# First layer's selective scan: decay kept in SBUF, B and C spread 1024 columns at a time, six of 48 y additions moved to VectorE

## The chip, the cores and the metric

The kernel runs on one core of one Trainium2 chip, as one launch. The metric is the device time in microseconds (us); three runs of the kernel before gave 1568.59 to 1570.61 with a median of 1569.81. TensorE does the matrix products, VectorE, ScalarE and GpSimd work on 128 partitions of SBUF (GpSimd reaches SBUF alone, the other two PSUM as well), and each engine runs its own instructions in order; semaphores tie the engines together. In the profile's rows PE is TensorE, PEld its weight load, DVE VectorE, ACT ScalarE, POOL GpSimd and SP the engine that issues most DMAs.

## The reference

A two-layer image model on an input of 4 x 48 x 64 x 64. The first layer's mixer is a selective scan in four directions (rows forward and back, columns forward and back) over 4096 positions, 96 channels, one state per channel. The change touches only this part:

```python
dts = jnp.einsum('bkrl,kdr->bkdl', dts_r, dt_projs_weight)
delta = jax.nn.softplus(dts + dt_projs_bias[None, :, :, None])
dA = jnp.exp(delta[..., None] * A[None, :, :, None, :])
dBu = delta[..., None] * Bt[:, :, None] * xs[..., None]
# h[t] = dA[t] * h[t-1] + dBu[t], by an associative scan
y = jnp.einsum('bkdln,bkln->bkdl', hs, Ct) + Ds.reshape(K, D_INNER)[None, :, :, None] * xs
# the four directions are turned back to image order and added up
```

After it come a norm, a projection, a small quantized feed-forward block, and the second layer (convolution, a 16-state scan, projection, feed-forward), which the change leaves alone.

## The kernel before

The program is five phases, one after the other: `front0_phase` (norm, convolution, the small projections), `scan0_phase` (this scan), `back0_phase`, `mid1_phase` (the second layer with its own, larger scan) and `back1_phase`.

`scan0_phase` puts 4 images x 32 channels on the 128 partitions and passes three times (`j`, J = 3) over the 96 channels. In each pass it walks four directions in the order of `order` (line 855): direction 2 (rows, backward), 1 (columns, forward), 3 (columns, backward), 0 (rows, forward). A direction is cut into NTC = 4 pieces of TC = 1024 positions. One piece in one direction is a *step*; there are 3 x 4 x 4 = 48 steps, 24 in row order and 24 in column order. A column step reads `z` and adds into `y` with a stride of 64 elements (`seen`, line 866), and has its own tiles in column order.

One step `i` goes like this:

- TensorE: two matmuls of 512 columns give the time step (`dt_of`, into `q_dt`), and two each spread B and C over the partitions (`spread`, into `q_b` and `q_c`, one bank of 512 columns each, so that the second half waits until VectorE has read the first).
- ScalarE: Softplus of `q_dt` into `dl` (`delta_of`), then Exp of `dl` times a per-channel scale into `q_a` (`decay`), which lies in PSUM, two buffers of 1024. It does two steps at a time, since the two functions need different tables.
- GpSimd: `u = dl * z` (line 1110), and two steps later `y += g` (line 1121). Both read two tiles of SBUF.
- VectorE: `u = u * q_b` in two halves (`drive`, line 1051), the scan `h` over 1024 positions from `q_a` and `u` (line 1062), and `g = h * q_c` of the step before in two halves (`times_c`, line 1073). Each of these reads one tile of SBUF and one of PSUM; where a direction goes on, the scan also takes its start value from the last column of the other `h`.

VectorE's order is written out (lines 1080 to 1088): first half of drive(i), first half of times_c(i-1), the second halves, then scan(i). GpSimd's is u(i), then y(i-2). `u`, `h`, `g` and `q_a` have two buffers, `dl` four, so u(i) waits for scan(i-2) and the product g(i) for y(i-2). `y` starts as `z` times a sum of D (`begin_y`, on ScalarE), and leaves by DMA after its last direction.

Of the kernel before, what the change touches and what calls it, by code (L numbers as in the profile page):

```python
# [21 lines left out]
ALU = mybir.AluOpType  # L22
# [808 lines left out]
def scan0_phase(nc, D, G, sems, past):  # L831

    with ExitStack() as scope:
# [14 lines left out]
        (y_begun, a_exp, a_ready, d_ready, dt_mm, b_mm, c_mm,  # L848
         delta, da_ready, u_ready, driven, scanned, read, added, y_stored) = (
            m.sem(f"b_{n}") for n in (  # L850
                "y_begun", "a_exp", "a_ready", "d_ready",
                "dt_mm", "b_mm", "c_mm", "delta", "da_ready", "u_ready", "driven", "scanned",
                "read", "added", "y_stored"))
# [31 lines left out]
        def from_rows(ap, col):  # L885

            return ap.rearrange("p (h w) -> p w h", h=H) if col else ap

        def by_column(ap, col):

            return ap.rearrange("p (w h) -> p w h", h=H) if col else ap
# [2 lines left out]

            return 2 * i + v + 1 + LEAD

        def in_order(back):

            return ((0, 1), (1, 0)) if back else ((0, 0), (1, 1))

        @block.sync
        def _(sp):
            def load_dt(k):
                for g, part in enumerate(X_PARTS):
                    sp.dma_start(dtx[k][DTR * g:DTR * g + DTR, :], D["dt0"][part, :, R0 * k:R0 * k + R0, :]).then_inc(dt_loaded[k], 16)
                sp.dma_start(dtx[k][BIAS_ROW:BIAS_ROW + 3, :], D["ones"].broadcast_to([3, T])).then_inc(dt_loaded[k], 16)

            def load_z(j):
                sp.dma_start(z[j % 2][:], D["z0"][j]).then_inc(z_loaded[j % 2], 16)

            def store(j):

                for c in range(NTC):
                    sp.wait_ge(added, done(n * j + 3 * NTC + c))
# [12 lines left out]
            load_z(1)  # L927
            for j in range(J):
                if j + 2 < J:
                    sp.wait_ge(u_ready, j * n + n + LEAD)  # L930
                    sp.wait_ge(y_begun, NTC * j + NTC)
                    load_z(j + 2)
                store(j)
            sp.wait_ge(y_stored, 16 * NTC * J)
            sp.nop(nofuse=True)

        @block.tensor
        def _(pe):
# [19 lines left out]
            def spread(j, st, o, q, row, used, ready):  # L958

                k, col, back, piece, first = steps[st]  # L960
                v = in_order(back)[o][1]

                if j * n + st < NTC:
                    pe.wait_ge(bc_first[piece], 16)
                pe.wait_ge(used, half(j * n + st, o) - 1)
                nc.tensor.matmul(in_rows(q[:], col), G["selbc0"][:, row + k, :],  # L966
                                 seen_rows(bcx[:], col, piece, v), start=True, stop=True).then_inc(ready, 1)

            def ahead(i, by):
                if i + by < last:  # L970
                    dt_of(i + by)

            dt_of(0)
            dt_of(1)
# [68 lines left out]
        def _(dve):  # L1043
            lead(dve, driven, scanned, read)

            def drive(i, s, o, v):
                part, col = slice(v * CH, v * CH + CH), steps[i % n][1]
                dve.wait_ge(u_ready, done(i))
                dve.wait_ge(b_mm, half(i, o))
                half_u = by_column(u[s][:, part], col)  # L1050
                nc.vector.tensor_tensor(half_u, half_u, from_rows(q_b[:], col), ALU.mult).then_inc(driven, 1)  # L1051

            def scan(i, s, back, first):
                way = slice(None, None, -1) if back else slice(None)
                dve.wait_ge(driven, half(i, 1))
                dve.wait_ge(da_ready, done(i))

                dve.wait_ge(scanned, done(i - 1))

                dve.wait_ge(read, half(i - 2, 1))  # L1060
# [4 lines left out]
            def times_c(i, o):  # L1065
                col, s = steps[i % n][1], i % 2
                v = in_order(steps[i % n][2])[o][1]
                part = slice(v * CH, v * CH + CH)
                dve.wait_ge(scanned, done(i))
                dve.wait_ge(c_mm, half(i, o))  # L1070

                dve.wait_ge(added, freed(i))
                nc.vector.tensor_tensor(by_column(g[s][:, part], col), by_column(h[s][:, part], col), from_rows(q_c[:], col),  # L1073
                                        ALU.mult).then_inc(read, 1)
# [12 lines left out]
            for o in range(2):  # L1087
                times_c(last - 1, o)

        @block.gpsimd  # L1090
        def _(pool):
# [7 lines left out]
            for i in range(last + 2):  # L1099
                if i < last:  # L1100
# [5 lines left out]
                    elif st == 0:  # L1106
# [1072 lines left out]
```

## Time and profile before

| | us |
|---|---|
| median of three runs | 1569.81 |
| the profiled execution | 1570.93 |
| its span in the profile | 1569.0 |
| first scan of this phase starts | 217.87 |
| last y addition of this phase ends | 474.23 |
| GpSimd busy from 236.7 to 466.6 | 229.90 |
| VectorE busy from 236.7 to 466.6 | 208.43 |
| ScalarE busy from 236.7 to 466.6 | 157.06 |
| TensorE busy from 236.7 to 466.6 | 136.29 |

The span is the stretch that the profiler recorded, 1.9 us less than the execution's own time, and that execution was 1.1 us above the median of the runs. TensorE's granted clock is 0.50 of full speed in all of the scan phase, the lower of its two levels. The last rows of the table add up what each engine was busy within a stretch; an engine that is busy for the whole of a stretch bounds it, one that is not waits for something. A duration in the trace holds everything from an instruction's start to its end, so one that has to wait after it has started shows the wait as part of its duration. Back-to-back instructions overlap a little: the time from the start of one to the start of the next is what one of them costs in a row of them.

### The profile page before, as it was taken

How to read it: one execution, taken by the hardware profiler on the slowest of the kernel's cores; microseconds unless marked ns; L12 is line 12 of the kernel's file. 1: busy time of each engine (PE TensorE's matmuls, PEld its weight loads, DVE VectorE, ACT ScalarE, POOL GpSimd, SP SyncE). 2: the span in 40 equal slices, each digit the busy share in tenths (PEclk: the TensorE clock that was granted, in tenths of full speed). 3: DMA queues.
4: the chain of work that ended last, by engine and by line, in shares of the span. 5: the costliest groups of instructions: out<-in, count | busy, mean ns of one | idle time of the engine just before them, and what ended most of it. 6: DMA issues, size and time to landing. Idle time of an engine off the chain costs nothing. (4 is left out here: it accounts for less than half of the span.)

```text
span 1569.0 us, 14783 instructions
## 1 busy us (share of the span) xinstructions
PE 1155.8 (74%) x3828; PEld 423.9 (27%) x3828; DVE 1205.6 (77%) x1198; ACT 1107.2 (71%) x1643; POOL 947.1 (60%) x501
## 2 busy tenths in 40 slices
PE   4899636665643777777888888888888888455995
PEld 2343101111102555422222222222222222002663
DVE  1666539998982777604999999999999999992775
ACT  2687257767642777648889889888888888741664
POOL 2500059999993333216988988888888889850000
PEclk8999855555556999978888888888888888666997
DMA  5455450301002233218878777788777886616572
GB/s 144 123 145 141 98 173 17 108 0 41 14 28 86 84 94 100 76 45 213 191 181 190 183 173 171 178 187 185 177 171 180 183 186 158 155 44 131 127 176 56
DMA packets 137487, 200.56 MB, mean 128 GB/s; under 512 B 27099, under 2 KB 69130, under 8 KB 136916
## 3 DMA queue, kind: packets, MB, share of 16 engines
q1 hardware_dynamic: 133964, 193.27, 50.1%
q0 software_dynamic: 1280, 3.74, 0.8%
q10 hardware_dynamic: 2160, 2.61, 0.7%
q8 instruction: 32, 0.52, 0.1%
q14 instruction: 51, 0.42, 0.1%
HBM read 145.93 MB, written 53.63 MB: 127 GB/s over the span
## 5 line engine op out<-in xcount | busy, mean ns | idle before, releaser
L1802 DVE TENSOR_TENSOR_SCAN m_h<-m_qa,m_state,m_ub 128x512 f32<-128x512 f32 x384 | 464.1, 1263 | 63.7 <-POOL m_ub L1389 56.9
L1389 POOL TENSOR_TENSOR m_ub<-m_dlb,m_bt 128x1536 f32<-128x1536 f32 x128 | 440.4, 3441 | 16.5 <-DMA m_dlb<-scratch_dldu 6.0
L1753 ACT ACTIVATE m_qa<-m_dlb,k_a 128x512 f32<-128x512 f32 x384 | 250.9, 681 | 56.7 <-DVE m_h L1802 52.1
L1813 DVE TENSOR_TENSOR m_g<-m_h,m_qc 128x1536 f32<-128x1536 f32 x128 | 221.4, 1730 | 10.0 <-DVE m_h L1802 8.6
L1596 PE MATMUL m_qm<-m_xa,k_u_taps 96*96 96x512 f32 x192 | 152.3, 959 | 32.3 <-ACT m_sz L1681 31.6
L1635 PE MATMUL m_qy<-m_g,k_seld 128*32 128x512 f32 x768 | 157.9, 697 | 0.0
L1110 POOL TENSOR_TENSOR b_u<-b_dl,b_z 128x1024 f32<-128x1024 f32 x48 | 130.3, 2714 | 17.9 <-ACT b_dl L1000 16.1
L1121 POOL TENSOR_TENSOR b_y<-b_y,b_g 128x1024 f32<-128x1024 f32 x48 | 135.9, 2830 | 3.4 <-DVE b_g L1073 3.2
L1618 PE MATMUL m_qc<-m_cp,k_selc 112*128 112x512 bf16 x128 | 52.3, 409 | 105.7 <-DVE m_g L1813 105.7
L966 PE MATMUL b_qb<-b_bc,k_pack_sel 96*128 96x512 bf16 x96 | 58.9, 613 | 94.8 <-DVE b_u L1051 94.7
L1411 POOL TENSOR_TENSOR m_rest<-m_bcr,m_cp 16x512 f32<-16x512 f32 x32 | 36.9, 1152 | 105.3 <-ACT m_cp L1722 76.1
L1051 DVE TENSOR_TENSOR b_u<-b_u,b_qb 128x512 f32<-128x512 f32 x96 | 65.3, 680 | 43.3 <-PE b_qb L966 29.8
L536 PE MATMUL n_q<-a_cv,k_conv 113*96 113x504 f32 (+1 forms) x192 | 91.9, 620 | 5.9 <-DVE a_acc L555 5.9
L1550 PE MATMUL m_qf<-m_cva,k_conv 113*96 113x504 f32 (+1 forms) x192 | 91.5, 614 | 4.9 <-PEq L1141 4.9
L1007 ACT ACTIVATE b_qa<-b_dl,b_a 128x1024 f32<-128x1024 f32 x48 | 53.6, 1118 | 58.5 <-DVE b_h L1062 58.3
L1062 DVE TENSOR_TENSOR_SCAN b_h<-b_qa,b_h,b_u 128x1024 f32<-128x1024 f32 x36 | 84.3, 2343 | 0.0
L1596 PEld LDWEIGHTS m_qm<-m_xa,k_u_taps 96*96 96x96 f32 x192 | 45.8, 257 | 138.8 <-issue 137.3
L1095 POOL DMA_DIRECT2D b_bc<-scratch_bc x4 | 2.3, 586 | 127.1 <-POOLq L577 127.1
L955 PE MATMUL b_qdt<-b_dt,b_wdt 75*128 75x512 bf16 x96 | 51.5, 622 | 33.2 <-DMA b_dt<-scratch_dt 24.5
L1000 ACT ACTIVATE b_dl<-b_qdt 128x512 f32<-128x512 f32 x96 | 52.1, 595 | 23.3 <-PE b_qdt L955 21.9
L1073 DVE TENSOR_TENSOR b_g<-b_h,b_qc 128x512 f32<-128x512 f32 x96 | 65.2, 679 | 1.0 <-PE b_qc L966 0.8
L1618 PEld LDWEIGHTS m_qc<-m_cp,k_selc 112*128 112x128 bf16 x128 | 12.9, 101 | 190.1 <-issue 188.3
(191 smaller groups left out, 2350.5 us busy)
## 6 DMA issues: line engine op xcount, KB each, us to landing
m_dlb<-scratch_dldu SPq DMA_DIRECT2D x128, 384.0 KB, 9.9
m_bt<-scratch_brow SPq DMA_DIRECT2D x128, 256.0 KB, 5.8
scratch_dldu<-m_dldu SPq DMA_DIRECT2D x32, 384.0 KB, 3.2
scratch_z<-a_z SPq DMA_DIRECT2D x24, 256.0 KB
scratch_y<-b_y SPq DMA_DIRECT2D x12, 512.0 KB, 2.6
c_y<-scratch_y SPq DMA_DIRECT2D x16, 384.0 KB, 3.4
scratch_gate<-m_gt SPq DMA_DIRECT2D x32, 192.0 KB, 3.7
scratch_y<-m_yo SPq DMA_DIRECT2D x32, 192.0 KB, 11.5
```

Of the source, the lines that this page charges most:

```text
L536: last = self.nc.tensor.matmul(out[:, :, o], self.pairs[:, tap, :], src[:, :, i], start=(tap == 1), stop=(tap == 2))
L1051: nc.vector.tensor_tensor(half_u, half_u, from_rows(q_b[:], col), ALU.mult).then_inc(driven, 1)
L1062: nc.vector.tensor_tensor_scan(h[s][:, way], q_a[s][:, way], u[s][:, way], carried, ALU.mult, ALU.add).then_inc(scanned, 1)
L1110: nc.gpsimd.tensor_tensor(by_column(u[s][:], col), by_column(dl[i % DL][:], col), seen(z[j % 2][:], col, piece), ALU.mult).then_inc(u_read ...
L1121: nc.gpsimd.tensor_tensor(part, part, by_column(g[i % 2][:], col), ALU.add).then_inc(added, 1)
L1389: nc.gpsimd.tensor_tensor(ub[k % 3][:], dlb[u % 2][:, J:2 * J, :], bcast(bt[u % 2][:, n, :], J), ALU.mult).then_inc(ub_ready, 1)
L1550: nc.tensor.matmul(out[:, :, o], G["conv1"][:, tap, :], src[:, :, i], start=(tap == 1), stop=False)
L1596: last = nc.tensor.matmul(q_m[:], G["u_taps"][:, k, :], xa[v % HIST][:, k:k + CH], start=(k == 0), stop=(k == 2))
L1635: last = nc.tensor.matmul(q_y[32 * j:32 * j + 32, :], G["seld"][:], g[k % 2][:, j, :], start=(n == 0), stop=(n == 3))
L1753: nc.scalar.activation(q_a[:, j, :], dlb[u % 2][:, j, :], ACT.Exp, scale=G["a1"][:, j, n:n + 1]).then_inc(da, 1)
L1802: nc.vector.tensor_tensor_scan(h[k % 3][:, j, :], q_a[:, j, :], ub[k % 3][:, j, :], state[:, k % NS, j:j + 1], ALU.mult, ALU.add).then_inc ...
L1813: nc.vector.tensor_tensor(g[k % 2][:], h[k % 3][:], bcast(q_c[:], J), ALU.mult).then_inc(read, 1)
```

## The change

Four edits, all in `scan0_phase`. The decay `qa` becomes an SBUF tile (two buffers of 1024). The four banks of PSUM that this frees make `q_b` two buffers of 1024 columns and `q_c` one of 1024. TensorE spreads B and C for a whole step (two matmuls, one signal), and B one step ahead. VectorE's drive and times_c become one instruction of 1024 each. And of the four steps of a column direction, the third one's `y += g` is done by VectorE (`add_y`, after scan(i+1)) and left out on GpSimd, with a semaphore of its own (`summed`): 2 column directions x 3 passes = 6 of 48 additions.

```diff
-        q_dt = m.ps("b_qdt", [P, TC])
-        q_b, q_c = m.ps("b_qb", [P, CH]), m.ps("b_qc", [P, CH])
-        q_a = [m.ps(f"b_qa{s}", [P, TC]) for s in range(2)]
+        qa = [m.sb(f"b_qa{s}", [P, TC]) for s in range(2)]
+        q_dt, q_c = m.ps("b_qdt", [P, TC]), m.ps("b_qc", [P, TC])
+        q_b = [m.ps(f"b_qb{s}", [P, TC]) for s in range(2)]
...
+        def by_vector(i):
+
+            return steps[i % n][1] and i % NTC == 2
...
+        def wait_direction(eng, i):
+
+            before = i - i % NTC - 1
+            if before >= 0:
+                eng.wait_ge(added, adds(before))
+                if sums(before) > 0:
+                    eng.wait_ge(summed, sums(before))
...
             for i in range(last + 1):
-                for o in range(2):
-                    if i < last:
-                        spread(i // n, i % n, o, q_b, 0, driven, b_mm)
-                    if i > 0:
-                        spread((i - 1) // n, (i - 1) % n, o, q_c, K4, read, c_mm)
-                    if o == 0 and i % 2 == 1:
-                        ahead(i, 2)
-                if i == 0:
+                b_of(i + 1)
+                if i == 0 or i % 2 == 1:
                     ahead(i, 2)
+                if i > 0:
+                    c_of(i - 1)
                 if i % 2 == 1:
                     ahead(i, 3)
...
-                nc.scalar.activation(q_a[i % 2][:], dl[i % DL][:], ACT.Exp, scale=a0[:, j, k:k + 1]).then_inc(da_ready, 1)
+                nc.scalar.activation(qa[i % 2][:], dl[i % DL][:], ACT.Exp, scale=a0[:, j, k:k + 1]).then_inc(da_ready, 1)
...
-                nc.vector.tensor_tensor_scan(h[s][:, way], q_a[s][:, way], u[s][:, way], carried,
+                nc.vector.tensor_tensor_scan(h[s][:, way], qa[s][:, way], u[s][:, way], carried,
                                              ALU.mult, ALU.add).then_inc(scanned, 1)
...
+            def add_y(i):
+                if not by_vector(i):
+                    return
+                k, col, back, piece, first = steps[i % n]
+                wait_direction(dve, i)
+                dve.wait_ge(read, done(i))
+                part = seen(y[i // n % 2][:], col, piece)
+                nc.vector.tensor_tensor(part, part, by_column(g[i % 2][:], col), ALU.add).then_inc(summed, 1)
...
-                for o, v in in_order(back):
-                    drive(i, i % 2, o, v)
-                    if i > 0:
-                        times_c(i - 1, o)
+                drive(i, i % 2)
+                if i > 0:
+                    times_c(i - 1)
                 scan(i, i % 2, back, first)
+                if i > 0:
+                    add_y(i - 1)
...
-                if i >= 2:
+                if i >= 2 and not by_vector(i - 2):
...
+                    wait_direction(pool, i - 2)
+                    if adds(i - 2) > LEAD + 1:
+                        pool.wait_ge(added, adds(i - 2) - 1)
```

On VectorE, at the end of the first column direction (steps 7 and 8): `b_u` is the driven input, `b_h` the scan's result, `b_g` the product with C, numbers are buffers, `b_qa` the decay, and the scan is listed as SCALAR_TENSOR_TENSOR. Before:

```order
L1051 TENSOR_TENSOR b_u1<-b_u1,b_qb 128x512 [waits b_b_mm,b_u_ready]
L1073 TENSOR_TENSOR b_g0<-b_h0,b_qc 128x512 [waits b_added,b_c_mm,b_scanned]
L1051 TENSOR_TENSOR b_u1<-b_u1,b_qb 128x512 [waits b_b_mm,b_u_ready]
L1073 TENSOR_TENSOR b_g0<-b_h0,b_qc 128x512 [waits b_added,b_c_mm,b_scanned]
L1062 SCALAR_TENSOR_TENSOR b_h1<-b_qa1,b_h0,b_u1 128x1024 [waits b_scanned,b_read,b_da_ready,b_driven]
```

The same place after the change, up to the next scan:

```order
L1087 TENSOR_TENSOR b_u1<-b_u1,b_qb1 128x1024 [waits b_b_mm,b_u_ready]
L1108 TENSOR_TENSOR b_g0<-b_h0,b_qc 128x1024 [waits b_added,b_c_mm,b_scanned]
L1098 SCALAR_TENSOR_TENSOR b_h1<-b_qa1,b_h0,b_u1 128x1024 [waits b_scanned,b_read,b_da_ready,b_driven]
L1118 TENSOR_TENSOR b_y0<-b_y0,b_g0 128x16x64 [waits b_read,b_added]
L1087 TENSOR_TENSOR b_u0<-b_u0,b_qb0 128x1024 [waits b_b_mm,b_u_ready]
L1108 TENSOR_TENSOR b_g1<-b_h1,b_qc 128x1024 [waits b_added,b_c_mm,b_scanned]
L1098 SCALAR_TENSOR_TENSOR b_h0<-b_qa0,b_u0 128x1024 [waits b_scanned,b_read,b_da_ready,b_driven]
```

Four half instructions became two whole ones, and the addition for step 6 stands behind scan(7). On GpSimd, over the same steps, before:

```order
L1121 TENSOR_TENSOR b_y0<-b_y0,b_g1 128x16x64 [waits b_added,b_read]
L1110 TENSOR_TENSOR b_u0<-b_dl0,b_z0 128x1024 [waits b_scanned,b_delta]
L1121 TENSOR_TENSOR b_y0<-b_y0,b_g0 128x16x64 [waits b_added,b_read]
L1110 TENSOR_TENSOR b_u1<-b_dl1,b_z0 128x1024 [waits b_scanned,b_delta]
L1121 TENSOR_TENSOR b_y0<-b_y0,b_g1 128x16x64 [waits b_added,b_read]
```

And with the change:

```order
L1167 TENSOR_TENSOR b_y0<-b_y0,b_g1 128x16x64 [waits b_added,b_read]
L1154 TENSOR_TENSOR b_u0<-b_dl0,b_z0 128x1024 [waits b_scanned,b_delta]
L1154 TENSOR_TENSOR b_u1<-b_dl1,b_z0 128x1024 [waits b_scanned,b_delta]
L1167 TENSOR_TENSOR b_y0<-b_y0,b_g1 128x16x64 [waits b_added,b_read]
L1154 TENSOR_TENSOR b_u0<-b_dl2,b_z0 128x1024 [waits b_scanned,b_delta]
```

Between the products for steps 8 and 9 the addition for step 6 is gone; everything else keeps its place. On TensorE, at an odd step (`b_qdt` is the time step's product, two matmuls), with the change:

```order
L995 MATMUL b_qb0<-b_bc,k_pack_sel 128x512 [waits b_driven]
L995 MATMUL b_qb0<-b_bc,k_pack_sel 128x512
L986 MATMUL b_qdt<-b_dt1,b_wdt 128x512 [waits b_delta] x2
L995 MATMUL b_qc<-b_bc,k_pack_sel 128x512 [waits b_read]
L995 MATMUL b_qc<-b_bc,k_pack_sel 128x512
L986 MATMUL b_qdt<-b_dt3,b_wdt 128x512 [waits b_delta,b_dt_loaded3]
```

There both matmuls of C stand behind a time-step product that waits for ScalarE; before, the first half of C stood ahead of it.

## Rows read from the trace of the kernel before

**Rows 1.** Busy time of each engine in the steady stretch (by --windows; x counts instructions).
```profile
core 0: us, PE busy (x) PEld busy (x) DVE busy (x) ACT busy (x) POOL busy (x), PEclk, DMA share, GB/s
236.70:466.60 229.90, 136.29 (x257) 26.32 (x256) 208.43 (x219) 157.06 (x178) 229.90 (x88) 0.50 0.09 33
```
**Rows 2.** GpSimd's timeline: start, duration, line, operation; idle before in brackets.
```profile
244.12 2.85 POOL L1110 TENSOR_TENSOR b_u<-b_dl,b_z 128x1024 f32<-128x1024 f32 x1
...
252.81 3.06 POOL L1121 TENSOR_TENSOR b_y<-b_y,b_g 128x1024 f32<-128x1024 f32 x1
255.83 2.84 POOL L1110 TENSOR_TENSOR b_u<-b_dl,b_z 128x1024 f32<-128x1024 f32 x1
...
279.14 2.41 POOL L1110 TENSOR_TENSOR b_u<-b_dl,b_z 128x1024 f32<-128x1024 f32 x1
...
289.80 2.42 POOL L1110 TENSOR_TENSOR b_u<-b_dl,b_z 128x1024 f32<-128x1024 f32 x1
...
317.49 2.95 POOL L1110 TENSOR_TENSOR b_u<-b_dl,b_z 128x1024 f32<-128x1024 f32 x1
...
471.89 2.34 POOL L1121 TENSOR_TENSOR b_y<-b_y,b_g 128x1024 f32<-128x1024 f32 x1 [2.10 <-DVE b_g L1073]
```
**Rows 3.** Waits from 226 to 467: who waited for whom, us, times, longest.
```profile
ACT b_qa L1007 <- DVE b_h L1062: 58.3, 23, 3.5
...
DVE b_u L1051 <- POOL b_u L1110: 13.5, 22, 0.9
DVE b_u L1051 <- PE b_qb L966: 8.7, 46, 0.8
```
**Rows 4.** VectorE's groups from 226 to 467: count, busy us, mean ns, idle before.
```profile
L1062 DVE TENSOR_TENSOR_SCAN b_h<-b_qa,b_h,b_u 128x1024 f32<-128x1024 f32 x35 | 82.0, 2343 | 0.0
L1051 DVE TENSOR_TENSOR b_u<-b_u,b_qb 128x512 f32<-128x512 f32 x92 | 62.6, 680 | 22.2 <-POOL b_u L1110 13.5 <-PE b_qb L966 8.7
L1073 DVE TENSOR_TENSOR b_g<-b_h,b_qc 128x512 f32<-128x512 f32 x92 | 62.5, 679 | 0.3 <-issue 0.3
```
**Rows 5.** VectorE's timeline: the second scan and the next instruction.
```profile
225.72 2.34 DVE L1062 TENSOR_TENSOR_SCAN b_h<-b_qa,b_h,b_u 128x1024 f32<-128x1024 f32 x1
227.99 0.66 DVE L1051 TENSOR_TENSOR b_u<-b_u,b_qb 128x512 f32<-128x512 f32 x1
```
**Rows 6.** The second layer's scan and GpSimd product: ns min/median/max.
```profile
L1802 DVE TENSOR_TENSOR_SCAN m_h<-m_qa,m_state,m_ub x384: 1251/1258/1284, 728.2 to 1411.0; 128x512 f32<-128x512 f32 x192
...
L1389 POOL TENSOR_TENSOR m_ub<-m_dlb,m_bt x128: 3410/3442/3472, 724.6 to 1396.8; 128x1536 f32<-128x1536 f32 x128
```
**Rows 7.** Line 555, first phase: ns min/median/max; n_q is PSUM, a_acc and a_low SBUF.
```profile
L555 DVE SCALAR_TENSOR_TENSOR a_acc<-a_low,k_pack_d,a_acc x64: 737/740/3453, 46.2 to 184.4; 96x504 f32<-96x504 f32 x64
L555 DVE SCALAR_TENSOR_TENSOR a_acc<-a_low,k_pack_d,n_q x32: 730/744/746, 45.4 to 182.9; 96x512 f32<-96x512 f32 x32
```
**Rows 8.** Timeline, first phase: one such VectorE instruction and the GpSimd one beside it.
```profile
47.44 3.40 POOL L200 TENSOR_TENSOR dtw<-dtw,dt_part 13x1536 f32<-13x1536 f32 x1
...
47.93 3.45 DVE L555 SCALAR_TENSOR_TENSOR a_acc<-a_low,k_pack_d,a_acc 96x504 f32<-96x504 f32 x1
```
**Rows 9.** Third phase: line 1286 overall (ns min/median/max), then a timeline; tiles in SBUF.
```profile
L1286 DVE TENSOR_TENSOR c_y<-c_y,c_yrs x16: 945/1444/1469, 491.1 to 645.0; 128x768 f32<-128x768 f32 x16
...
624.30 0.72 POOL L1169 TENSOR_TENSOR c_ys<-c_y 128x256 f32<-128x256 f32 x1 [2.44 <-DMA c_xin<-in_x]
624.65 1.19 DVE L1286 TENSOR_TENSOR c_y<-c_y,c_yrs 128x768 f32<-128x768 f32 x1 [0.16 <-ACT c_yrs L1270]
625.11 1.32 POOL L1171 TENSOR_TENSOR c_ys<-c_ys,c_y 128x256 f32<-128x256 f32 x1
```
**Rows 10.** VectorE products of 1536 and 1024 columns, one input in PSUM: mean ns.
```profile
L1813 DVE TENSOR_TENSOR m_g<-m_h,m_qc 128x1536 f32<-128x1536 f32 x128 | 221.4, 1730 | 10.0 <-DVE m_h L1802 8.6 <-issue 0.8
...
L1906 DVE TENSOR_TENSOR g_y<-g_q,g_gt 96x1024 f32<-96x1024 f32 x16 | 19.4, 1213 | 24.9 <-PE g_q L1875 24.9
```

More of the change, by code:

```diff
@@ L844, in scan0_phase @@
         u, h, g = ([m.sb(f"b_{n}{s}", [P, TC]) for s in range(2)] for n in ("u", "h", "g"))
-        q_dt = m.ps("b_qdt", [P, TC])
-        q_b, q_c = m.ps("b_qb", [P, CH]), m.ps("b_qc", [P, CH])
-        q_a = [m.ps(f"b_qa{s}", [P, TC]) for s in range(2)]
+        qa = [m.sb(f"b_qa{s}", [P, TC]) for s in range(2)]
+        q_dt, q_c = m.ps("b_qdt", [P, TC]), m.ps("b_qc", [P, TC])
+        q_b = [m.ps(f"b_qb{s}", [P, TC]) for s in range(2)]
         (y_begun, a_exp, a_ready, d_ready, dt_mm, b_mm, c_mm,
-         delta, da_ready, u_ready, driven, scanned, read, added, y_stored) = (
+         delta, da_ready, u_ready, driven, scanned, read, added, summed, y_stored) = (
             m.sem(f"b_{n}") for n in (
@@ L852, in scan0_phase @@
                 "dt_mm", "b_mm", "c_mm", "delta", "da_ready", "u_ready", "driven", "scanned",
-                "read", "added", "y_stored"))
+                "read", "added", "summed", "y_stored"))
         order = [(2, 0, 1), (1, 1, 0), (3, 1, 1), (0, 0, 0)]
@@ L887, in from_rows, with halves_from_rows, halves_by_column @@
             return ap.rearrange("p (h w) -> p w h", h=H) if col else ap
+        def halves_from_rows(ap, col):
+            return ap.rearrange("p (v h w) -> p v w h", v=TC // CH, h=H) if col else ap
+        def halves_by_column(ap, col):
+            return ap.rearrange("p (v w h) -> p v w h", v=TC // CH, h=H) if col else ap
         def by_column(ap, col):
@@ L895, in half, with sums, adds, wait_added @@
             return 2 * i + v + 1 + LEAD
-        def in_order(back):
-            return ((0, 1), (1, 0)) if back else ((0, 0), (1, 1))
+        def by_vector(i):
+            return steps[i % n][1] and i % NTC == 2
+        def sums(i):
+            return sum(by_vector(e) for e in range(i + 1))
+        def adds(i):
+            return LEAD + i + 1 - sums(i)
+        def wait_added(eng, i):
+            if by_vector(i):
+                eng.wait_ge(summed, sums(i))
+            else:
+                eng.wait_ge(added, adds(i))
+        def wait_direction(eng, i):
[4 more added lines that the diff above has]
+                    eng.wait_ge(summed, sums(before))
         @block.sync
@@ L913, in store @@
                 for c in range(NTC):
-                    sp.wait_ge(added, done(n * j + 3 * NTC + c))
+                    wait_added(sp, n * j + 3 * NTC + c)
                     sp.nop(nofuse=True)
@@ L956, in dt_of, with spread, b_of, c_of @@
                                      seen_rows(dtx[k][:], col, piece, v), start=True, stop=True).then_inc(dt_mm, 1)
[L958 to L963, printed above, removed]
+            def spread(i, q, row, ready):
+                k, col, back, piece, first = steps[i % n]
+                if i < NTC:
                     pe.wait_ge(bc_first[piece], 16)
-                pe.wait_ge(used, half(j * n + st, o) - 1)
-                nc.tensor.matmul(in_rows(q[:], col), G["selbc0"][:, row + k, :],
-                                 seen_rows(bcx[:], col, piece, v), start=True, stop=True).then_inc(ready, 1)
+                for v in range(TC // CH):
+                    last = nc.tensor.matmul(in_rows(q[:, v * CH:v * CH + CH], col), G["selbc0"][:, row + k, :],
+                                            seen_rows(bcx[:], col, piece, v), start=True, stop=True)
+                last.then_inc(ready, 1)
+            def b_of(i):
+                if i < last:
+                    pe.wait_ge(driven, freed(i))
+                    spread(i, q_b[i % 2], 0, b_mm)
+            def c_of(i):
+                pe.wait_ge(read, freed(i, 1))
+                spread(i, q_c, K4, c_mm)
             def ahead(i, by):
@@ L973, in _ @@
             dt_of(0)
+            b_of(0)
             dt_of(1)
             for i in range(last + 1):
[L976 to L983 removed]
+                b_of(i + 1)
+                if i == 0 or i % 2 == 1:
                     ahead(i, 2)
+                if i > 0:
+                    c_of(i - 1)
                 if i % 2 == 1:
@@ L1044, in _, with drive @@
             lead(dve, driven, scanned, read)
-            def drive(i, s, o, v):
-                part, col = slice(v * CH, v * CH + CH), steps[i % n][1]
+            def drive(i, s):
+                col = steps[i % n][1]
                 dve.wait_ge(u_ready, done(i))
-                dve.wait_ge(b_mm, half(i, o))
-                half_u = by_column(u[s][:, part], col)
-                nc.vector.tensor_tensor(half_u, half_u, from_rows(q_b[:], col), ALU.mult).then_inc(driven, 1)
+                dve.wait_ge(b_mm, done(i))
+                whole_u = halves_by_column(u[s][:], col)
+                nc.vector.tensor_tensor(whole_u, whole_u, halves_from_rows(q_b[s][:], col), ALU.mult).then_inc(driven, 1)
@@ L1053, in scan @@
             def scan(i, s, back, first):
                 way = slice(None, None, -1) if back else slice(None)
-                dve.wait_ge(driven, half(i, 1))
+                dve.wait_ge(driven, done(i))
                 dve.wait_ge(da_ready, done(i))
                 dve.wait_ge(scanned, done(i - 1))
-                dve.wait_ge(read, half(i - 2, 1))
+                dve.wait_ge(read, done(i - 2))
                 carried = 0.0 if first else h[1 - s][:, 0:1] if back else h[1 - s][:, TC - 1:TC]
-                nc.vector.tensor_tensor_scan(h[s][:, way], q_a[s][:, way], u[s][:, way], carried,
+                nc.vector.tensor_tensor_scan(h[s][:, way], qa[s][:, way], u[s][:, way], carried,
@@ L1063, in scan, with times_c @@
                                              ALU.mult, ALU.add).then_inc(scanned, 1)
-            def times_c(i, o):
+            def times_c(i):
                 col, s = steps[i % n][1], i % 2
-                v = in_order(steps[i % n][2])[o][1]
-                part = slice(v * CH, v * CH + CH)
                 dve.wait_ge(scanned, done(i))
[L1070 to L1074, printed above, removed]
+                dve.wait_ge(c_mm, done(i))
+                if i >= 2:
+                    wait_added(dve, i - 2)
+                nc.vector.tensor_tensor(halves_by_column(g[s][:], col), halves_by_column(h[s][:], col),
+                                        halves_from_rows(q_c[:], col), ALU.mult).then_inc(read, 1)
@@ L1076, in _ @@
+            def add_y(i):
+                if not by_vector(i):
+                    return
+                k, col, back, piece, first = steps[i % n]
+                wait_direction(dve, i)
+                dve.wait_ge(read, done(i))
+                part = seen(y[i // n % 2][:], col, piece)
+                nc.vector.tensor_tensor(part, part, by_column(g[i % 2][:], col), ALU.add).then_inc(summed, 1)
             dve.wait_ge(a_loaded, 32)
@@ L1081, in _ @@
                 back, first = steps[i % n][2], steps[i % n][4]
-                for o, v in in_order(back):
-                    drive(i, i % 2, o, v)
-                    if i > 0:
-                        times_c(i - 1, o)
+                drive(i, i % 2)
+                if i > 0:
+                    times_c(i - 1)
                 scan(i, i % 2, back, first)
-            for o in range(2):
-                times_c(last - 1, o)
+                if i > 0:
+                    add_y(i - 1)
+            times_c(last - 1)
         @block.gpsimd
@@ L1116, in _ @@
                         pool.wait_ge(y_begun, NTC * j + st + 1)
-                    pool.wait_ge(read, half(i - 2, 1))
-                    pool.wait_ge(added, done(i - 3))
+                    pool.wait_ge(read, done(i - 2))
+                    wait_direction(pool, i - 2)
+                    if adds(i - 2) > LEAD + 1:
+                        pool.wait_ge(added, adds(i - 2) - 1)
                     part = seen(y[j % 2][:], col, piece)
```

## The prediction, made before the run

> **What bounds the kernel now.** I read the busy times of the scan stretch first, then GpSimd's timeline, the waits and VectorE's groups, and last the places elsewhere in the program where VectorE and GpSimd meet on SBUF tiles.
>
> From 236.7 to 466.6 us GpSimd is busy for all 229.90 us of 229.90, VectorE for 208.43, ScalarE for 157.06, TensorE for 136.29 [rows 1]. So GpSimd sets the pace of this phase, and its timeline gives its prices, start to start [rows 2]. In a row stretch, from 289.80 to 317.49, stand 12 instructions: 27.69 / 12 = 2.31 us each. In a column stretch, from 244.12 to 279.14, stand six pairs: 35.02 / 6 = 5.84 a pair, of which the addition takes 255.83 - 252.81 = 3.02 and the product `u` the other 2.82. The last addition ends at 471.89 + 2.34 = 474.2.
>
> The others wait for it or for what it feeds: VectorE's drive waits 13.5 us for `u`, ScalarE's Exp 58.3 us for a scan [rows 3]. VectorE's scan takes 2.34 us, 2.27 from its start to the next instruction's [rows 4, 5], a half product 0.68. In a step it has 2.27 and four halves, no more than 5.0 us: under GpSimd's 5.84 in column steps, a little over its 2.31 x 2 = 4.62 in row steps.
>
> **The change, part by part.** *Whole products.* Of 1024 columns with one PSUM input a product takes about 1.21 us [rows 10], and 1.73 at 1536 columns. Two per step are 2.42 for 4 x 0.68 = 2.72: 0.30 x 48 = 14 us less VectorE time. It lies beside GpSimd's work and gains nothing while GpSimd is the bound.
>
> *B and C spread ahead.* The number of matmuls stays. The 8.7 us that VectorE waited for B [rows 3] can go; GpSimd is late next, so nothing by itself. If GpSimd were not the cover, this and the whole products would be worth 8.7 and 14 us in VectorE's row steps at most.
>
> *New waits.* `add_y(i)` waits for the additions of the direction before; on GpSimd those stand ahead of u(i), which VectorE needed for its drive(i) long before. GpSimd's first addition of a direction waits for the VectorE addition of the one before; VectorE does that ahead of the product g which the same GpSimd addition needs anyway. Neither can end last, so what is queued behind them (the next `u`, the next drive) is not held.
>
> *Six additions leave GpSimd.* 6 x 3.02 = 18.1 us off the bound. On VectorE each is a 1024-column sum with strided y. No row shows one: below it stands 1.21 (contiguous, rows 10), above it GpSimd's own 3.06 [rows 2]. I take 1.21 x 3.02 / 2.31 = 1.6, VectorE's price with the factor that the stride costs GpSimd: 9.6 us for six.
>
> The Trainium skill, "Vector Engine (DVE) Microarchitecture Reference", section 5.2, gives 1.7 to 2.5 ns a column where an operand hops every element; as an estimate that is 1.8 to 2.6 us each, and the sum below would rise by 1 to 6 us. No run here shows it.
>
> *The decay in SBUF.* This is what I expect to decide the time. Before, the scan read one SBUF tile (`u`) and one PSUM tile. Now it reads two SBUF tiles, and so does `add_y`. GpSimd's two instructions always read two. What the trace shows of such pairs:
>
> - One SBUF input beside GpSimd: no effect. The second layer's scans run from 1251 to 1284 ns while GpSimd's products run beside them in 3410 to 3472 [rows 6]; this phase's half products average 680 and 679 [rows 4].
> - Two SBUF inputs: line 555 with PSUM as one input takes 730 to 746 ns in every case, with both in SBUF 737 to 3453 [rows 7]. The 3.45 us one starts at 47.93, in a GpSimd instruction that ends at 50.84, and ends at 51.38, 0.54 after it [rows 8]. Alone it takes 0.74, so it stood still for nearly all of the GpSimd instruction.
> - The other way round too: line 1286, 0.945 us alone, starts at 624.65, waits for the GpSimd addition that ends at 625.02 and ends at 625.84; the next GpSimd addition, issued at 625.11, takes 1.32 instead of 0.72 and ends 0.59 after VectorE's [rows 9]. The one that waited got in between two GpSimd instructions.
>
> So the two exclude each other for whole instructions. The Trainium skill, "SBUF — State Buffer", section "Who interferes with whom", says just that: a VectorE instruction with two SBUF inputs contends with a GpSimd one that reads SBUF, and whichever comes second is fully blocked. By that rule the scan must take turns with GpSimd, and the trace agrees for the two operations with such rows (3.45 against 0.74 us); of a scan it has no row with two SBUF inputs.
>
> If the scans take turns with GpSimd, the phase lasts as long as the sum of both, whatever the order. In every step the scan leaves GpSimd a `u` and a `y` to do, and VectorE's two products (2.42 us) fit beside one or the other, so the shared resource doesn't fall idle; whether VectorE gets in after one GpSimd instruction or after two, a step costs scan + u + y: 2.27 + 4.62 = 6.89 in row steps, 2.27 + 5.84 = 8.11 in column steps. TensorE and ScalarE, at 136 and 157 us of 230, stay hidden, and the C product's later place costs nothing.
>
> The sum, from the second scan's start at 225.72, which I leave where it is (up to there the change adds one C matmul, tenths of a us): 47 scans x 2.27 = 106.7; GpSimd's 21 `u` and 24 `y` of row steps x 2.31 = 104.0; 24 column pairs x 5.84 = 140.2; less 18.1; six VectorE additions 9.6. Together 342.4. The last addition ends at 225.7 + 342.4 = 568.1 instead of 474.2: 93.9 us later. What follows is unchanged. The profiled execution took 1570.9, so 1664.8; it lay 1.1 over the median of the runs, which gives 1664.
>
> Its bounds. Down: in the blocked cases part of the duration was already spent while waiting, 0.54 shown of 0.74 [rows 7, 8] and 0.59 of 0.72 [rows 9]. A scan then holds 2.34 - 0.20 = 2.14 (6 us less over 47), one GpSimd instruction a step 2.34 - 0.13 = 2.21 (5 less), an addition 1.21 (2 less): 1651. Up: full durations instead of start to start, 0.07 x 47 + 0.03 x 93 = 6; additions at 3.06, 9 more; a wake-up of 0.16 a step, as VectorE shows behind ScalarE [rows 9], 8 more: 1687.
>
> **Rivals.** *Faster: the scan is not held.* One mechanism, at line 1098, and it decides for all 47 scans at once: a scan uses two ns per column, so its second input may come another way than that of a product. For it: no row shows such a scan, and all scans so far ran undisturbed [rows 4, 6]. Against it: line 555 is also a two-step operation on two SBUF tiles and was held. GpSimd then stays the bound with 18.1 us less to do; VectorE needs 2.27 + 2.42 in a row step, like GpSimd: 1569.8 - 18.1 = 1552. Chance 0.08.
>
> *No change: the scan is not held, but C comes late.* In odd steps both C matmuls now stand behind a time-step product that waits for Softplus. If VectorE waited there as long as its longest wait for B, 0.8 us [rows 3], in 24 odd steps, 19 us would eat the 18.1. It decides only where GpSimd has no slack left. 1570; chance 0.02.
>
> *Half the price: they slow each other down instead of taking turns.* Then half of the scans' and additions' 116.3 us might be lost: 1552 + 58 = 1610. For it: a scan asks for a column only every 2 ns. Against it: rows 8 and 9 show standing still and no slowing. Chance 0.05.
>
> **How the numbers follow.** Forecast (turns taken) 0.85, range 1651 to 1687. A measurement of this kernel can tell 0.2%, some 3 us, from no change. Slower by more: 0.85 + 0.05 = 0.90; faster 0.08; within 0.02. The range for 8 in 10 has to take nearly all of the first case, so I widen its bounds a little, 1640 to 1692; the half price and the two cases without a hold stay outside.
>
> **What would show it.** In the changed profile the scan's mean should rise from 2.34 to between 3 and 5 us with maxima near 2.3 + 3, and GpSimd's `u` and `y` from 2.7 and 2.8 towards 4, both with waiting inside their durations; drive and times_c should stay at 1.2. `add_y` should show several us where a GpSimd instruction runs. GpSimd should still look busy throughout a phase that is some 94 us longer, and every other phase should keep its length. I would be wrong if scans stay at 2.34 beside GpSimd (then the time is near 1552), if scans lengthen but GpSimd's instructions do not and it has idle time (then it is another wait), or if the phase is longer while VectorE waits for C.

## The result, and the profile after

The changed kernel takes **1653.18 us** (median of 4 runs, 1649.85 to 1655.67) beside 1570.21 for the kernel before in the same series: a ratio of **1.0521, with 95% interval 1.049 to 1.0553**. It is slower by 83 us, where 94 were forecast, and inside the range. The profiled execution took 1651.93 us, its span is 1650.0.

All of it lies in the scan phase. The last `y` addition ended at 474.23 before and ends at 554.44 + 2.34 = 556.78 now, 82.6 us later; from there to the end of the span it was 1094.8 us before and is 1093.2 now.

Busy time of each engine in the steady stretch, 313.20 us long, as in [rows 1]:

```profile
core 0: us, PE busy (x) PEld busy (x) DVE busy (x) ACT busy (x) POOL busy (x), PEclk, DMA share, GB/s
236.70:549.90 313.20, 121.94 (x253) 22.64 (x252) 282.55 (x139) 157.22 (x178) 312.53 (x82) 0.50 0.06 23
```

GpSimd looks as full as before, 312.53 of 313.20, yet needs 83 us more for less work. Which instructions became longer is in the groups of the stretch from 226 to 556 (count, busy us, mean ns, idle us before and its releaser):

```profile
L1167 POOL TENSOR_TENSOR b_y<-b_y,b_g 128x1024 f32<-128x1024 f32 x42 | 169.3, 4032 | 1.4 <-DVE b_g L1108 1.2 <-POOL b_y L1167 0.2
L1154 POOL TENSOR_TENSOR b_u<-b_dl,b_z 128x1024 f32<-128x1024 f32 x45 | 164.7, 3665 | 0.0
L1098 DVE TENSOR_TENSOR_SCAN b_h<-b_qa,b_h,b_u 128x1024 f32<-128x1024 f32 x36 | 130.5, 3626 | 0.0
L1108 DVE TENSOR_TENSOR b_g<-b_h,b_qc 128x1024 f32<-128x1024 f32 x47 | 56.8, 1208 | 0.0
L1087 DVE TENSOR_TENSOR b_u<-b_u,b_qb 128x1024 f32<-128x1024 f32 x46 | 55.1, 1198 | 30.7 <-POOL b_u L1154 30.7
```

The scan rose from a mean of 2343 ns [rows 4] to 3626; GpSimd's two kinds, 2.34 to 3.06 us before [rows 2], to means of 4032 and 3665. VectorE's products, which read one PSUM input, are at their 1.2 us. No new wait explains it: GpSimd, which sets the pace, is idle for 1.4 us. VectorE waits 30.7 us for `u` (13.5 before) and not at all for B or C, ScalarE's Exp 121.7 us for scans (58.3 before [rows 3]). The loss is inside the durations. The smallest, median and largest of each (ns), by line:

```profile
L1098 DVE TENSOR_TENSOR_SCAN b_h<-b_qa,b_h,b_u x36: 2340/2892/4956, 224.8 to 549.8; 128x1024 f32<-128x1024 f32 x36
...
L1118 DVE TENSOR_TENSOR b_y<-b_y,b_g x6: 4341/4597/4853, 267.9 to 525.0; 128x1024 f32<-128x1024 f32 x6
...
L1154 POOL TENSOR_TENSOR b_u<-b_dl,b_z x48: 2332/3548/4882, 209.6 to 543.1; 128x1024 f32<-128x1024 f32 x48
...
L1167 POOL TENSOR_TENSOR b_y<-b_y,b_g x42: 2337/4342/5083, 225.0 to 554.4; 128x1024 f32<-128x1024 f32 x42
```

The smallest of the scans and of GpSimd's two kinds is the old price, the largest that price and most of the other engine's instruction on top. The timeline of a row stretch shows how one runs into the other (start, duration, engine, line, operation):

```profile
316.31 2.34 POOL L1154 TENSOR_TENSOR b_u<-b_dl,b_z 128x1024 f32<-128x1024 f32 x1
316.34 4.47 DVE L1098 TENSOR_TENSOR_SCAN b_h<-b_qa,b_h,b_u 128x1024 f32<-128x1024 f32 x1
318.62 4.34 POOL L1167 TENSOR_TENSOR b_y<-b_y,b_g 128x1024 f32<-128x1024 f32 x1
320.72 1.19 DVE L1087 TENSOR_TENSOR b_u<-b_u,b_qb 128x1024 f32<-128x1024 f32 x1
321.84 1.21 DVE L1108 TENSOR_TENSOR b_g<-b_h,b_qc 128x1024 f32<-128x1024 f32 x1
322.92 2.34 POOL L1154 TENSOR_TENSOR b_u<-b_dl,b_z 128x1024 f32<-128x1024 f32 x1
322.97 4.44 DVE L1098 TENSOR_TENSOR_SCAN b_h<-b_qa,b_h,b_u 128x1024 f32<-128x1024 f32 x1
...
349.33 2.85 POOL L1154 TENSOR_TENSOR b_u<-b_dl,b_z 128x1024 f32<-128x1024 f32 x1
```

The scan of 316.34 starts while `u` runs. `u` ends at 318.65, the scan at 320.81, 2.16 us after it. `y`, issued at 318.62, stands still meanwhile and ends at 322.96, 2.15 after the scan; beside it VectorE does its two products at full speed. Then the pattern repeats. From 316.31 to 349.33 are five steps: 6.60 us each, where GpSimd alone took 2 x 2.31 = 4.62 [rows 2]. So a scan adds 1.98.

### The profile page after: what moved, and what is told of

It is laid out like the page before. It is cut to its first block and busy times, and to the rows that moved or that the text cites. A ratio compares the mean times of both kernels' runs of the same rounds, so it can differ in the third digit from the quotient of the medians.

```text
span 1650.0 us, 14619 instructions
## 1 busy us (share of the span) xinstructions
PE 1151.3 (70%) x3828; PEld 420.8 (26%) x3828; DVE 1279.1 (78%) x1108; ACT 1107.8 (67%) x1643; POOL 1033.5 (63%) x495
## 3 DMA queue, kind: packets, MB, share of 16 engines
q10 hardware_dynamic: 2160, 2.61, 0.7%
## 5 line engine op out<-in xcount | busy, mean ns | idle before, releaser
L1799 ACT ACTIVATE m_qa<-m_dlb,k_a 128x512 f32<-128x512 f32 x384 | 250.8, 681 | 54.5 <-DVE m_h L1848 50.5
L1154 POOL TENSOR_TENSOR b_u<-b_dl,b_z 128x1024 f32<-128x1024 f32 x48 | 171.7, 3582 | 17.2 <-ACT b_dl L1036 15.0
L1642 PE MATMUL m_qm<-m_xa,k_u_taps 96*96 96x512 f32 x192 | 156.2, 981 | 30.3 <-ACT m_sz L1727 29.6
L1167 POOL TENSOR_TENSOR b_y<-b_y,b_g 128x1024 f32<-128x1024 f32 x42 | 169.3, 4032 | 1.4 <-DVE b_g L1108 1.2
L995 PE MATMUL b_qb<-b_bc,k_pack_sel 96*128 96x512 bf16 x96 | 49.8, 622 | 169.6 <-DVE b_u L1087 169.6
L1681 PE MATMUL m_qy<-m_g,k_seld 128*32 128x512 f32 x768 | 162.8, 716 | 0.0
L1043 ACT ACTIVATE b_qa<-b_dl,b_a 128x1024 f32<-128x1024 f32 x48 | 55.0, 1149 | 121.9 <-DVE b_h L1098 121.7
L1098 DVE TENSOR_TENSOR_SCAN b_h<-b_qa,b_h,b_u 128x1024 f32<-128x1024 f32 x36 | 130.5, 3626 | 0.0
L1087 DVE TENSOR_TENSOR b_u<-b_u,b_qb 128x1024 f32<-128x1024 f32 x48 | 57.5, 1199 | 45.8 <-POOL b_u L1154 45.8
L1215 POOL TENSOR_TENSOR c_ys<-c_ysq 128x256 f32<-128x256 f32 x16 | 11.6, 724 | 82.6 <-ACT c_ysq L1310 82.6
```

The lines of the kernel that those rows point to most:

```text
L1098: nc.vector.tensor_tensor_scan(h[s][:, way], qa[s][:, way], u[s][:, way], carried, ALU.mult, ALU.add).then_inc(scanned, 1)
L1642: last = nc.tensor.matmul(q_m[:], G["u_taps"][:, k, :], xa[v % HIST][:, k:k + CH], start=(k == 0), stop=(k == 2))
L1681: last = nc.tensor.matmul(q_y[32 * j:32 * j + 32, :], G["seld"][:], g[k % 2][:, j, :], start=(n == 0), stop=(n == 3))
L1799: nc.scalar.activation(q_a[:, j, :], dlb[u % 2][:, j, :], ACT.Exp, scale=G["a1"][:, j, n:n + 1]).then_inc(da, 1)
```

## The experiments

The phase's start shifts by up to 5 us between executions, for reasons ahead of it, so beside the totals I give the phase's length in the profiled execution, from GpSimd's first `u` to the end of the last `y`. Ratios are to the kernel before on the same chip, where its median was 1567.81 us (1 to 4), 1569.28 (5 to 7) and 1570.96 (8 and 9).

| kernel | us | ratio, 95% interval | phase, us |
|---|---|---|---|
| before | 1570.21 | 1 | 262.9 |
| after | 1653.18 | 1.0521 (1.049 to 1.0553) | 347.1 |
| 1 only the decay in SBUF | 1659.88 | 1.0579 (1.0553 to 1.0606) | 353.9 |
| 2 after, no VectorE additions | 1655.96 | 1.0564 (1.0532 to 1.0596) | 353.1 |
| 3 after, driven input in PSUM | 1573.78 | 1.0038 (1.0014 to 1.0062) | 266.4 |
| 4 as 3, no VectorE additions | 1564.88 | 0.9981 (0.9967 to 0.9995) | 260.8 |
| 5 before, with VectorE additions | 1576.67 | 1.0029 (1.0007 to 1.0052) | 269.7 |
| 6 as 3, added product in PSUM | 1557.56 | 0.9901 (0.9867 to 0.9935) | 248.6 |
| 7 as 3, addition ahead of the scan | 1575.91 | 1.0029 (1.0007 to 1.005) | 267.0 |
| 8 as 6, `u` freed by the drive | 1552.75 | 0.9887 (0.9869 to 0.9905) | 246.9 |
| 9 as 8, nine additions | 1557.36 | 0.9922 (0.9895 to 0.9949) | 250.8 |

**1. Only the decay in SBUF.** One line of the kernel before:

```diff
-        q_a = [m.ps(f"b_qa{s}", [P, TC]) for s in range(2)]
+        q_a = [m.sb(f"b_qa{s}", [P, TC]) for s in range(2)]
```

> The kernel before with one edit: the decay tile in SBUF instead of PSUM; half products, single B and C banks and all 48 additions on GpSimd stay. Theory (a scan with two SBUF inputs takes turns with GpSimd): in the changed kernel a row step lasted 6.60 us, so a scan holds GpSimd up for 6.60 - 4.62 = 1.98; 47 x 1.98 = 93 us on top of GpSimd's 244, end of the phase near 563 instead of 474: about 1659. Rival (the time of the changed kernel comes from its whole-step spreads, the later C product or the additions on VectorE): no difference, 1570, scans at 2.34.

1659.88: this line alone brings the whole loss. The scans by line (ns, smallest, median, largest):

```profile
L1062 DVE TENSOR_TENSOR_SCAN b_h<-b_qa,b_h,b_u x36: 2345/2514/7858, 225.9 to 558.1; 128x1024 f32<-128x1024 f32 x36
L1062 DVE TENSOR_TENSOR_SCAN b_h<-b_qa,b_u x12: 2284/2494/4567, 218.0 to 536.9; 128x1024 f32<-128x1024 f32 x12
```

The median is only 0.17 above the old price: here it is mostly GpSimd that stands still. One scan waited for longer than any in the changed kernel, 7.86 us; its place in the timeline:

```profile
410.68 3.14 POOL L1121 TENSOR_TENSOR b_y<-b_y,b_g 128x1024 f32<-128x1024 f32 x1
...
413.41 7.86 DVE L1062 TENSOR_TENSOR_SCAN b_h<-b_qa,b_h,b_u 128x1024 f32<-128x1024 f32 x1
...
413.73 2.38 POOL L1110 TENSOR_TENSOR b_u<-b_dl,b_z 128x1024 f32<-128x1024 f32 x1
416.02 3.10 POOL L1121 TENSOR_TENSOR b_y<-b_y,b_g 128x1024 f32<-128x1024 f32 x1
...
421.41 2.35 POOL L1110 TENSOR_TENSOR b_u<-b_dl,b_z 128x1024 f32<-128x1024 f32 x1 [2.29 <-DVE b_h L1062]
```

It began while a `y` ran, which ended at 413.82. Then `u` and the next `y` went ahead of it at their full speed, and it ended 2.15 after the second (419.12, 421.27). GpSimd, with nothing left that it could do before this scan's end, was idle for 2.29. That cost little: from the `u` of 413.73 two steps last 15.22 us, and the same two steps of the other passes 14.65 and 14.63. So a scan that lets two instructions pass costs 0.6 us more here, close to the nothing that the prediction had for it.

**2. All additions back on GpSimd.** After, with one line changed:

```diff
-            return steps[i % n][1] and i % NTC == 2
+            return False
```

> The changed kernel with all 48 additions back on GpSimd; decay in SBUF and whole products stay. Theory: an addition on VectorE holds GpSimd up for about 1.5 us and saves it 3.02, so giving six back costs 6 x 1.5 = 9 us: about 1662. Rival (the 4.3 to 4.9 us that these additions show are time on the path): 6 x (4.6 - 3.0) = 10 us less, about 1643.

The totals, 1655.96 and 1653.18, don't tell the two kernels apart, and they match neither number expected. The phase does tell them apart, 353.1 beside 347.1, but in one profiled execution of each, and that of 2 is the slowest of its four (1663.35 us). The step lengths of the two traces agree with it: with an addition on VectorE, two steps take 14.54 us in the first column direction (265.78 to 280.32) and 13.67 in the second, without it 15.66 and 14.62. So six additions moved to VectorE save 6.0 us, 1.0 each: 3.02 on GpSimd against 2.0 of excluded time on VectorE, where 1.5 was expected. Whole products and the early B and C, all that is left between kernels 1 and 2, are worth 353.9 - 353.1 = 0.8 at most, about the nothing that was forecast; about 0.6 of it is the long scan of 1.

**3. The driven input in PSUM.** After, with decay still in SBUF; `q_b` gives up a buffer, and the C matmuls go ahead of the next B:

```diff
-        q_b = [m.ps(f"b_qb{s}", [P, TC]) for s in range(2)]
+        q_b, q_u = m.ps("b_qb", [P, TC]), m.ps("b_qu", [P, TC])
...
+                if i > 0:
+                    dve.wait_ge(scanned, done(i - 1))
-                nc.vector.tensor_tensor(whole_u, whole_u, halves_from_rows(q_b[s][:], col), ALU.mult).then_inc(driven, 1)
+                nc.vector.tensor_tensor(halves_by_column(q_u[:], col), whole_u, halves_from_rows(q_b[:], col), ALU.mult).then_inc(driven, 1)
...
-                nc.vector.tensor_tensor_scan(h[s][:, way], qa[s][:, way], u[s][:, way], carried,
+                nc.vector.tensor_tensor_scan(h[s][:, way], qa[s][:, way], q_u[:, way], carried,
```

> The changed kernel, but VectorE writes the driven input (u times B) to a PSUM tile, so that the scan reads one SBUF tile (the decay) and one PSUM tile; B has one buffer of 1024 columns instead of two, and C is spread ahead of the next B. Theory: it is the number of SBUF inputs that counts, so scans are back at 2.34 and GpSimd is the bound with 18 us less to do, of which the additions on VectorE still hold it up for 9: about 1561. Rival (the decay in SBUF or the whole-step spreads cost the time in another way): near 1650. A third outcome: with one buffer of B VectorE waits about 1.2 us a step for it: about 1595.

The 83 us are gone, but the time missed 1561 by 13: the additions, which still read two SBUF tiles, gave their gain back. Their durations, and the first of them with GpSimd's timeline:

```profile
L1122 DVE TENSOR_TENSOR b_y<-b_y,b_g x6: 2930/5696/6221, 259.7 to 453.2; 128x1024 f32<-128x1024 f32 x6
```

```profile
258.18 2.86 POOL L1158 TENSOR_TENSOR b_u<-b_dl,b_z 128x1024 f32<-128x1024 f32 x1
...
259.74 6.22 DVE L1122 TENSOR_TENSOR b_y<-b_y,b_g 128x1024 f32<-128x1024 f32 x1
...
260.99 2.86 POOL L1158 TENSOR_TENSOR b_u<-b_dl,b_z 128x1024 f32<-128x1024 f32 x1
...
268.28 3.08 POOL L1171 TENSOR_TENSOR b_y<-b_y,b_g 128x1024 f32<-128x1024 f32 x1 [4.43 <-DVE b_g L1112]
```

It started in the first `u`, and the second went ahead of it, both unhindered at 2.86. The addition ended 2.11 after the second one; VectorE's next product came after it, and GpSimd had to wait 4.43 for `g`. GpSimd's waits for `g` are 21.2 us in all, more than the 18.1 saved.

**4. As 3, no VectorE additions** (the edit of 2).

> As the kernel with the driven input in PSUM, but all 48 additions on GpSimd. No VectorE instruction of the phase then has two SBUF inputs. Theory: GpSimd is the bound with the work that it had before, 1570, and the whole products gain nothing since they lie beside it. Rival (VectorE was the bound in row steps, where it had 5.0 us against 4.6): up to 24 x 0.3 = 7 us less, 1563.

1564.88, between the two numbers expected and nearer the rival's. The rival's reason isn't borne out: GpSimd's 12 instructions from 288.46 to 316.18 take 27.72 us, as the 12 before took 27.69 [rows 2]. Of the 2.1 us by which the phase is shorter than before, 1.6 lie behind GpSimd's last `u`, where GpSimd waits for VectorE's last scan and product. The scans:

```profile
L1102 DVE TENSOR_TENSOR_SCAN b_h<-b_qa,b_h,b_qu x36: 2341/2341/2342, 222.1 to 465.4; 128x1024 f32<-128x1024 f32 x36
```

The decay is in SBUF as in the changed kernel, GpSimd works beside these scans, and the shortest and the longest differ by 1 ns. Before, the scan had `u` in SBUF and the decay in PSUM; here it is the other way round, and neither holds it. It is the second SBUF input that holds a scan, not the decay's place or GpSimd's load.

**5. Before, with the six VectorE additions alone** (`by_vector`, `add_y` and `summed` as in the change's diff).

> The kernel before with one edit: six of the 48 additions on VectorE, placed as in the change; decay in PSUM, half products. Only these six VectorE instructions then have two SBUF inputs. Theory: each saves GpSimd 3.02 us and holds it up for 2.1 (the hold seen in the changed kernel), 6 us less at best, but with the driven input in PSUM some of them stood still behind two GpSimd instructions and the kernel lost 9 us against the one without them; the same here gives 1570 to 1577. Rival (the additions simply move work off the bound): 1570 - 18 = 1552.

1576.67: in the kernel before, too, the additions alone bring nothing and cost a little. The cause is that of 3: 2.48 to 5.58 us each, and GpSimd waits 22.4 us for `g`.

**6. As 3, the added product kept in PSUM.** In the six steps times_c writes its product over C in `q_c`, and the addition right behind it reads it from there, in row order of `y`:

```diff
+                product = halves_from_rows(q_c[:], col) if by_vector(i) else halves_by_column(g[s][:], col)
...
-                nc.vector.tensor_tensor(part, part, by_column(g[i % 2][:], col), ALU.add).then_inc(summed, 1)
+                nc.vector.tensor_tensor(part, part, q_c[:].rearrange("p (v h w) -> p v h w", v=TC // CH, h=H),
+                                        ALU.add).then_inc(summed, 1)
```

> The kernel with the driven input in PSUM, and for the six steps whose addition VectorE does the product with C is written over C in PSUM and added to y in row order right behind it, so that no VectorE instruction of the phase has two SBUF inputs. Theory: now the 18.1 us of GpSimd's additions come off the bound with nothing in return: 1565 - 18 = 1547. Rival (VectorE with 4.5 us a step and six additions becomes the bound, or C comes late behind the addition): 1555 to 1565.

1557.56, 12 us under before: not the 1547 of the theory, but in the rival's range. The addition:

```profile
L1127 DVE TENSOR_TENSOR b_y<-b_y,b_qc x6: 1221/1222/1222, 252.9 to 431.5; 128x1024 f32<-128x1024 f32 x6
```

1.22 us in all six, beside GpSimd: without a second SBUF input and in row order it costs what a product does. The phase is 12.2 shorter than in 4, where 18.1 were to be had. Most of the 5.9 between is GpSimd's idle time: 3.4 ahead of `u`, for scans, and 3.3 ahead of `y`, where 4 has 0.1 and 1.5.

**7. As 3, the addition ahead of the scan** (`add_y(i - 1)` moved above `scan`).

> The kernel with the driven input in PSUM, but with each VectorE addition ahead of the scan of the next step instead of behind it; it still reads two SBUF tiles. Theory (a waiting VectorE instruction gets its turn whenever GpSimd ends one): additions at most 2.8 + 2.1 = 4.9 us, GpSimd's gain of 6 us shows: about 1560. Rival (GpSimd keeps its turn over back-to-back instructions): additions of 6 us and more remain in some steps, 1570 to 1577.

The rival was right: 1575.91, additions of 2.61 to 5.47, and now GpSimd waits 18.3 us for scans. The order on VectorE doesn't give the addition its turn.

**8. As 6, GpSimd's `u(i)` waits for the drive two steps before, not for its scan**, which no longer reads `u`:

```diff
-                    pool.wait_ge(scanned, freed(i))
+                    pool.wait_ge(driven, freed(i))
```

> The kernel with the added product in PSUM, and GpSimd's next product may overwrite u once drive has read it, where it waited for the scan: in the kernel before this edit GpSimd waited 3.4 us for scans, in the six steps with an addition on VectorE. Theory: these 3.4 us go, 1 to 4 us less than that kernel's 1557.6, and the phase is about 245 us from the first product to the last addition (248.5 before this edit). Rival (VectorE is late there anyway, and GpSimd waits for g instead): no change.

1552.75, the fastest kernel here, 18 us under before. The wait for scans is gone, the phase 1.7 shorter than in 6; in the totals that step isn't resolved, as the intervals overlap.

**9. As 8, a third piece in the last row direction too: nine additions.**

```diff
-            return steps[i % n][1] and i % NTC == 2
+            return i % NTC == 2 and (steps[i % n][1] or i % n > 2 * NTC)
```

`add_y` gets a branch for row order, where it takes `q_c` as it lies.

> As the kernel with u freed by drive, with three more additions on VectorE (the third piece of the last, row-order direction): nine of 48. Theory: GpSimd has 3 x 2.31 = 6.9 us less, VectorE 3 x 1.2 = 3.6 more and comes close to being the bound in row steps (4.5 against 4.6 us a step): 2 to 5 us less. Rival (VectorE is the bound in row steps): up to 3 us more.

The rival again: 1557.36, no gain, and the phase 3.9 longer. GpSimd's waits, of this kernel and then of 8 (total us, times, longest):

```profile
POOL b_y L1179 <- DVE b_g L1115: 16.4, 6, 6.8
```

```profile
POOL b_y L1176 <- DVE b_g L1115: 5.8, 5, 1.9
```

VectorE in the last row direction of the second pass:

```profile
384.85 1.23 DVE L1093 TENSOR_TENSOR b_qu<-b_u,b_qb 128x1024 f32<-128x1024 f32 x1
...
387.11 2.34 DVE L1104 TENSOR_TENSOR_SCAN b_h<-b_qa,b_h,b_qu 128x1024 f32<-128x1024 f32 x1
389.59 1.23 DVE L1093 TENSOR_TENSOR b_qu<-b_u,b_qb 128x1024 f32<-128x1024 f32 x1
...
394.33 1.23 DVE L1093 TENSOR_TENSOR b_qu<-b_u,b_qb 128x1024 f32<-128x1024 f32 x1
```

Start to start a row step costs it 4.74 (384.85, 389.59, 394.33), with no wait listed, against GpSimd's 4.62. The drive starts 2.48 after the scan, not 2.27 as before [rows 5]: it now overwrites the tile that the scan reads, and waits for the scan's end. So VectorE is the bound in row steps, and three additions of 1.2 more there account for about 3.6 of the 3.9.

## Why the prediction was right, step by step

**The mechanism** held in each part. The scan takes turns with GpSimd for whole instructions (timeline of 316 to 323); one line brings it (1), and one input moved to PSUM takes it away (4). The Trainium skill, "SBUF — State Buffer", section "Who interferes with whom", says that of two such instructions the second is blocked until the first is done. The trace agrees, now for a scan too: up to 4.96 us against 2.34. It also shows more than that: in 1, 3, 5 and 7 some blocked instructions stood through a second one (last section). The rival without a hold (1552) and that of half the price (1610) fall with it. A late C would show as VectorE waiting at line 1108, and there is 0.0 of that.

**The sum** was 342.4 us from the second scan's start and is 556.78 - 224.82 = 332.0. Two of its terms were mis-sized:

- *The scan's hold.* I took 2.27 a scan, the whole time from its start to the next instruction's. Measured are 1.98 in row steps, and as much in column steps, from 280.32 to 288.14 in this timeline: 7.82 - 5.84.

```profile
280.32 4.86 POOL L1154 TENSOR_TENSOR b_u<-b_dl,b_z 128x1024 f32<-128x1024 f32 x1
285.13 3.10 POOL L1167 TENSOR_TENSOR b_y<-b_y,b_g 128x1024 f32<-128x1024 f32 x1
...
288.14 4.88 POOL L1154 TENSOR_TENSOR b_u<-b_dl,b_z 128x1024 f32<-128x1024 f32 x1
```

 Part of a blocked instruction's duration passes while it stands, and that holds on both sides: the scan ends 2.16 after `u` instead of 2.34, `y` 2.15 after the scan instead of 2.34. The rows on lines 555 and 1286 [rows 7 to 9] had shown it, and I had it as the lower bound: 2.14 for a scan and 2.21 for one GpSimd instruction a step, together 2.14 - 0.10 = 2.04. The measured value lies 0.06 below even that. I took 0.29 x 47 = 13.6 us too much.

- *The additions.* I took 1.6 each, with 1.21 below and 3.06 above. The one of 381.34:

```profile
379.23 4.83 POOL L1154 TENSOR_TENSOR b_u<-b_dl,b_z 128x1024 f32<-128x1024 f32 x1
...
381.34 4.85 DVE L1118 TENSOR_TENSOR b_y<-b_y,b_g 128x1024 f32<-128x1024 f32 x1
...
384.02 4.76 POOL L1154 TENSOR_TENSOR b_u<-b_dl,b_z 128x1024 f32<-128x1024 f32 x1
```

 `u` ends at 384.06 and the addition at 386.19: 2.13. As with the scan, the GpSimd instruction behind it is shorter in turn, and 2.0 is left on the path (2). That is 0.4 x 6 = 2.4 too little. The estimate from the Trainium skill, "Vector Engine (DVE) Microarchitecture Reference", section 5.2, was 1.8 to 2.6 for a strided operand; the trace agrees with 2.0 and 2.13. In 6, with `y` in runs of 8 neighbours and the product from PSUM, it is 1.22.

342.4 - 13.6 + 2.4 = 331.2, against 332.0; 0.8 stays open. The two errors go opposite ways, so the additions hid a little of the scans' error. The second scan started 0.9 earlier than before (224.82 against 225.72 [rows 5]), the stretch behind the phase is 1.6 shorter in this execution, and these with the 10.4 make the 12.9 between 1664.8 and 1651.9.

**Costed at nothing, rightly:** whole products and the earlier B and C under GpSimd's cover (0.8 us at most, by 1 and 2); the new waits (GpSimd idle 1.4 us in 330).

**Not seen:** that the 18.1 us of the additions would not have come even without the held scans. My rival of 1552 had them as pure gain, and 3 and 5 show that in SBUF they are lost to VectorE's standing still and GpSimd's wait for `g`. It took 6 and 8 to get most of them: 13.9 us of the phase, beside 4.

## What to carry to other kernels

Before moving a tile from PSUM to SBUF, count the SBUF inputs of every VectorE instruction that reads it while GpSimd works on SBUF: the second one turns parallel work into a sum, here 1.98 us for each scan of 2.34, and it shows only as longer durations, with both engines looking busy. The cure is to keep one input of each such instruction in PSUM, and to place a VectorE addition where its other operand already lies there. Work moved off the engine that bounds pays only while the receiving engine has slack in that very stretch: six additions did, nine did not.

## What was not expected of the hardware

A VectorE instruction that waits doesn't always get in when the GpSimd one ahead of it ends. In the changed kernel all six additions got in behind the instruction that they had met (4.34 to 4.85 us). In 3, 5 and 7, 11 of 18 stood through another whole GpSimd instruction (4.93 to 6.22 us; the other seven took 2.48 to 2.95), and so did the scan of 7.86 us in 1. It repeats from pass to pass: all nine additions of the first column direction stood (6.22, 6.22 and 6.21 in 3), of the second only two of nine, so it is hardly chance. What decides who goes next stays open: moving the addition ahead of the scan (7) didn't change it, and no run tried it by itself.
